# Best-32 attention with quads two to a turn behind the scores, and the state kernel in quarters

## The reference, cut to what matters

```python
s = q @ k.T / sqrt(32)              # per head, 128 queries x 4096 keys at a time
kth = top_k(s, 32)[..., -1:]
p = softmax(where(s >= kth, s, -inf))
c0 = mean_over_heads(p) @ context
K[d, l] = 2 * real(sum_n(dC[d, n] * exp(dtA[d, n] * l)))
```

## Time and profile before

| | us |
|---|---|
| median of 3 runs | 1250.7 (1249.63 to 1252.78) |
| profiled execution, time | 1249.94 |
| profiled execution, span | 1248.7 |
| PE busy | 1023.1 (82%) |
| DVE busy | 835.4 (67%) |
| ACT busy | 627.9 (50%) |
| POOL busy | 253.1 (20%) |

### The profile page before, as it was taken

The page is one execution under the profiler, slowest core; times in us unless marked ns, Lnnn a source line. Parts: engine busy times, 40 slices in busy tenths (PEclk is TensorE's granted clock), DMA queues, the critical chain, the costliest instruction groups (busy, mean ns, idle before and its releaser), DMA issues. The chain is left out here.

```text
span 1248.7 us, 20560 instructions
## 1 busy us (share of the span) xinstructions
PE 1023.1 (82%) x7560; PEld 624.6 (50%) x7560; DVE 835.4 (67%) x1812; ACT 627.9 (50%) x1014; POOL 253.1 (20%) x276
## 2 busy tenths in 40 slices
PE   6988589999999999868799782587787778973877
PEld 5877434444444444438455461335545456442564
DVE  5677689999999998036334559988485744533472
ACT  4434138787887888613311140799696882011100
POOL 1000488895000000000000010073434330000100
PEclk9999769999999999967799876667877789977855
DMA  6777522223222221010122270014521155003200
GB/s 207 273 260 270 185 66 77 78 77 84 76 76 80 76 76 39 10 53 1 52 89 76 80 187 5 1 56 115 139 78 51 39 156 186 0 1 84 68 1 17
DMA packets 97993, 110.63 MB, mean 89 GB/s; under 512 B 26475, under 2 KB 74404, under 8 KB 97892
## 3 DMA queue, kind: packets, MB, share of 16 engines
q1 hardware_dynamic: 95572, 108.52, 28.9%
q10 hardware_dynamic: 2320, 0.79, 0.3%
HBM read 79.77 MB, written 29.43 MB: 87 GB/s over the span
## 5 line engine op out<-in xcount | busy, mean ns | idle before, releaser
L806 ACT ACTIVATE pT<-bank 128x512 f32<-128x512 f32 x512 | 278.4, 597 | 94.6 <-PE bank L745 73.2
L827 DVE TENSOR_REDUCE rmax<-bank 128x2 f32<-128x1024 f32 x256 | 307.4, 1223 | 19.1 <-PE bank L713 18.1
L1547 PE MATMUL bank<-K1s,qs 97*128 97x512 f32 x256 | 137.2, 629 | 56.0 <-ACT below L1653 36.6
L757 PE MATMUL bank<-pT,V 128*17 128x256 f32 x2048 | 161.8, 388 | 4.7 <-ACT oT L812 4.6
L745 PEld LDWEIGHTS bank<-qs,ks 49*128 49x128 f32 x1024 | 78.1, 187 | 113.8 <-ACT pT L806 100.8
L1810 POOL TENSOR_TENSOR total<-total,work 128x1024 f32<-128x1024 f32 x40 | 94.7, 2375 | 194.9 <-ACT work L1662 194.5
L745 PE MATMUL bank<-qs,ks 49*128 49x256 f32 x1024 | 130.5, 333 | 2.5 <-ACT pT L806 0.5
L713 PE MATMUL bank<-ks,qs 49*128 49x512 f32 x512 | 111.2, 429 | 16.2 <-DMA ks<-k_parts_d 9.0
L1547 PEld LDWEIGHTS bank<-K1s,qs 97*128 97x128 f32 x256 | 61.1, 250 | 72.7 <-ACT below L1653 37.3
L1717 DVE MAX8 cand<-work 128x8 f32<-128x128 f32 x384 | 77.5, 279 | 0.0
L1662 ACT ACTIVATE work<-bank,ebias 128x1024 f32<-128x1024 f32 x48 | 53.6, 1120 | 31.7 <-PE bank L1550 31.7
(11 more groups left out here) (432 smaller groups left out, 1870.2 us busy)
## 6 DMA issues: line engine op xcount, KB each, us to landing
k_parts_d<-kparts SPq DMA_DIRECT2D x48, 512.0 KB, 3.6
ks<-k_parts_d SPq DMA_DIRECT2D x384, 64.0 KB, 2.2
K1s<-k_parts_d SPq DMA_DIRECT2D x96, 128.0 KB
cn<-in_ctx SPq DMA_DIRECT2D x32, 384.0 KB, 3.4
cx<-in_ctx SPq DMA_DIRECT2D x16, 384.0 KB
w<-in_L_ffn_w SPq DMA_DIRECT2D x32, 128.0 KB
w2e<-in_L_ffn_w SPq DMA_DIRECT2D x16, 128.0 KB
W<-in_L_xattn_W SPq DMA_DIRECT2D x2, 1024.0 KB, 7.4
```

Source lines behind the costliest of these rows:

```text
L757: t = pe.matmul(bank[32 * c:32 * c + VW, 7, a * S:(a + 1) * S], V[:, b * NCH + 4 * g + c, h, :], pT[:, (at + 2 * (c // 2) + a) % 8, c % 2 ...
L806: p_made.up(act.activation(pT[:, at % 8, :], bank[:, 4 + at % 3, :], ACT.Exp))
L827: max_read.up(dve.tensor_reduce(rmax[p % 2][:, :, qt, c], bank[:, b0:b0 + 2, :], AX.X, ALU.max))
L1547: m = pe.matmul(bank[:, b0 + c, :], qs1[0:NROW1, b * H1 + h, q], K1s[h][0:NROW1, keys], start=True, stop=(what == "new"))
```

## The change: what it does, and the diff

Seven edits, all in this stage. (1) `quads` becomes a table over quarters g = 4s + k: groups 0 and 1 get two quads per turn (quarters 0 and 2) in turns 6 to 9 and 10 to 13, group 2 gets two in turn 14, four in turn 15 and two in turn 16. (2) PE's loop puts the scores of a quarter first, then the weighing of the quad of the quarter before, then the turning of the next quarter's quad (where two quads follow on each other, of this quarter's). (3) The state kernel is made in four quarters, the first in bank 2 ahead of the turning in `prep_tensor`, the others one sixteenth per quarter turn in turns 0 to 2 in bank 7; its copies move accordingly. (4) `sum_over` moves from quarter 0 to quarter 1, with DVE's cast behind the candidates of quarter 1. (5) ACT runs `mark_below` before `sum_best`, and spreads `sum_best`, `log_sum` and `exp_bias` over quarters 1 to 3. (6) At the end DVE does one late add before `copy_c0` of group 2. (7) SP issues the context loads by the new table. The hunks that only move declarations (`kst`, the K flags) are left out below.

```diff
@@ -1316,6 +1316,26 @@
+    kst = [a.rearrange("p i d -> p (i d)").rearrange("p (a g) -> p a g", a=LA) for a in (xn[:, :, :], xT[:, :, :])]
+    K_made, K_copied, K_stored = flag("K_made"), flag("K_copied"), flag("K_stored")
+    def kernel_sixteenth(at, k_bank):
+        for i in range(4 * at, 4 * at + 4):
+            hs, g = slice(i // 32 * NSTATE, (i // 32 + 1) * NSTATE), i % 32
+            for c in range(2):
+                for q in range(4):
+                    m = pe.matmul(bank[32 * q:32 * q + LB, k_bank, i % 16 * LA:(i % 16 + 1) * LA],
+                                  Bp[c][hs, q, :, g], Ap[c][hs, q, :, g], start=(c == 0), stop=(c == 1))
+        if at % 4 == 3:
+            K_made.up(m)
+    def copy_kernel(n, k_bank):
+        act.wait_ge(*K_made.at(n + 1))
+        K_copied.up(act.copy(kst[n // 2][:, :, n % 2 * 16:n % 2 * 16 + 16].rearrange("p a g -> p g a"),
+                             bank[:, k_bank, :].rearrange("p (g a) -> p g a", a=LA)))
@@ -1343,6 +1363,9 @@
     def prep_tensor():
+        pe.wait_ge(*powers_made.at(1))
+        for at in range(4):
+            kernel_sixteenth(at, 2)
         pe.wait_ge(*ln_made.at(4 * 4))
@@ -1356,6 +1379,7 @@
         turn_scalar(4)
+        copy_kernel(0, 2)
         norm_scalar(4)
@@ -1443,13 +1465,19 @@
 
-    def quads(s):
-        grp, k = (s - 6) // H1, (s - 6) % H1
-        return [(grp, n) for n in ((0, 1), (2, 3, 4), (5, 6, 7), ())[k]] if s >= 6 and grp < NGRP - 1 else []
-    K_SHARE = (2, 1, 1)
+    quads = {}
+    for grp in range(NGRP - 1):
+        first = 4 * grp + 6
+        spots = [(first + j // 2, j % 2 * 2) for j in range(NQ)]
+        if grp == NGRP - 2:
+            spots = [(first, 0), (first, 2)] + [(first + 1, k) for k in range(4)] + [(first + 2, k) for k in range(2)]
+        for n, (s, k) in enumerate(spots):
+            quads[4 * s + k] = (grp, n)
+    K_FROM, K_BANK = 4, 7
 
@@ -1490,9 +1518,10 @@
                     vecs_in.up(sp.dma_start(vecs[:, k, :], row("L1_xattn_" + n).to_broadcast([P, D])), 16)
-            for _ in quads(s):
-                load_context(at)
-                at += 1
+            for k in range(4):
+                if 4 * s + k in quads:
+                    load_context(at)
+                    at += 1
         after_cut(LAST - 1)
@@ -1511,26 +1540,6 @@
     def best_tensor():
-        made = [0]
-        def kernel_share(n):
-            for at in range(4 * made[0], 4 * (made[0] + n)):
-                if at % 16 == 0:
-                    if at:
-                        pe.wait_ge(*K_copied.at(at // 16))
-                    else:
-                        pe.wait_ge(*powers_made.at(1))
-                        pe.wait_ge(*q1_low.at(H1))
-                hs, g = slice(at // 32 * NSTATE, (at // 32 + 1) * NSTATE), at % 32
-                for c in range(2):
-                    for q in range(4):
-                        m = pe.matmul(bank[32 * q:32 * q + LB, 7, at % 16 * LA:(at % 16 + 1) * LA],
-                                      Bp[c][hs, q, :, g], Ap[c][hs, q, :, g], start=(c == 0), stop=(c == 1))
-                if at % 16 == 15:
-                    K_made.up(m)
-            made[0] += n
@@ -1554,7 +1563,7 @@
                 pe.wait_ge(*over_in.at(t))
-            pe.wait_ge(*aT_made.at(sum(len(quads(s)) for s in range(t + 1))))
+            pe.wait_ge(*aT_made.at(total_turned.n))
             over_summed.up(pe.matmul(bank[0:1, 6, 0:1], over[:, :], ones[:, 0:1], start=True, stop=True))
@@ -1565,7 +1574,7 @@
                 pe.wait_ge(*aT_made.at(at))
-            pe.wait_ge(*over_in.at(min(NTL, 4 * grp + 6 + (n >= 2) + (n >= 5))))
+            pe.wait_ge(*over_in.at(over_summed.n))
             for c in range(4):
@@ -1585,24 +1594,28 @@
         for k in range(4):
+            if k == 1:
+                pe.wait_ge(*K_copied.at(1))
             if k == 2:
         pe.wait_ge(*minus_made.at(1))
-        for s in range(NTL + 1):
-            for k in range(4):
-                for what in pieces_of(s, k):
-                    piece(*what)
-                if k == 0 and 1 <= s <= NTL:
-                    sum_over(s - 1)
-                if s < len(K_SHARE):
-                    kernel_share(K_SHARE[s])
-                if 1 <= k <= len(quads(s)):
-                    turn_quad(*quads(s)[k - 1])
-                if 2 <= k <= len(quads(s)) + 1:
-                    weigh_quad(*quads(s)[k - 2])
-            if len(quads(s)) == 3:
-                weigh_quad(*quads(s)[2])
+        for g in range(4 * (NTL + 1)):
+            s, k = g // 4, g % 4
+            for what in pieces_of(s, k):
+                piece(*what)
+            if s and k == (s < NTL):
+                sum_over(s - 1)
+            if g < 12:
+                if g % 4 == 0:
+                    pe.wait_ge(*K_copied.at(g // 4 + 1))
+                kernel_sixteenth(K_FROM + g, K_BANK)
+            if g - 1 in quads:
+                weigh_quad(*quads[g - 1])
+            if g in quads and g - 1 in quads:
+                turn_quad(*quads[g])
+            if g + 1 in quads and g not in quads:
+                turn_quad(*quads[g + 1])
         piece("cut", LAST, 3)
@@ -1631,7 +1644,6 @@
             j = t % 2
-            act.wait_ge(*picked.at(t + 1))
             e_summed.up(act.activation(etop[:, :], top[j][:, :], ACT.Exp, bias=ntop[:, j:j + 1], accum_out=ssum[:, j:j + 1]))
@@ -1670,11 +1682,6 @@
-        def copy_kernel(n):
-            act.wait_ge(*K_made.at(n + 1))
-            K_copied.up(act.copy(kst[n // 2][:, :, n % 2 * 16:n % 2 * 16 + 16].rearrange("p a g -> p g a"),
-                                 bank[:, 7, :].rearrange("p (g a) -> p g a", a=LA)))
 
@@ -1686,23 +1693,25 @@
                         exps(t, piece)
-                if 1 <= s <= NTL:
+                if 1 <= s < NTL:
+                    if k % 2:
+                        mark_below(s - 1, k - 1, 2)
+                    if k == 1:
+                        sum_best(s - 1)
+                    if k == 2:
+                        log_sum(s - 1)
+                    if k == 3:
+                        exp_bias(s - 1)
+                if s == NTL:
+                    mark_below(s - 1, k, 1)
                     if k == 0:
                         sum_best(s - 1)
-                    if s == NTL:
-                        mark_below(s - 1, k, 1)
-                    elif k % 2:
-                        mark_below(s - 1, k - 1, 2)
-                    if k == 0:
                         log_sum(s - 1)
-                    if k == (s < NTL):
                         exp_bias(s - 1)
-                if s < len(K_SHARE):
-                    share = sum(4 * n for n in K_SHARE[:s]) + K_SHARE[s] * (k + 1)
-                    if share % 4 == 0:
-                        copy_kernel(share // 4 - 1)
-                if 1 <= k <= len(quads(s)):
-                    copy_quad(*quads(s)[k - 1])
+                if s < 3 and k == 3:
+                    copy_kernel(s + 1, K_BANK)
+                if 4 * s + k in quads:
+                    copy_quad(*quads[4 * s + k])
         exps(LAST, 3)
@@ -1781,9 +1790,8 @@
                     candidates(s, k)
-                if k == 0 and 1 <= s <= NTL:
+                if k == (s < NTL) and 1 <= s <= NTL:
                     over_to_sbuf(s - 1)
-                if k == (s < NTL) and 1 <= s <= NTL:
                     settle(s - 1)
@@ -1792,10 +1800,12 @@
                 copy_c0((s - 9) // H1)
-        for t, grp in ((LATE, NGRP - 2), (LAST, NGRP - 1)):
+        for t in (LATE, LAST):
             for k in range(4):
                 add_late(t, k)
-            copy_c0(grp)
+                if (t, k) == (LAST, 0):
+                    copy_c0(NGRP - 2)
+        copy_c0(NGRP - 1)
 
```

More of the change, by code:

```diff
@@ L1406, in build @@
     c0 = xn[:, :, 0:DC]
-    kst = [a.rearrange("p i d -> p (i d)").rearrange("p (a g) -> p a g", a=LA) for a in (xn[:, :, :], xT[:, :, :])]
     ctxn_d = ins["ctx_768"].rearrange("b (c p) d -> b p c d", p=P)
@@ L1419, in build @@
         "total_turned", "aT_made", "c0_made", "c0_copied", "tm_in", "tmask_made", "c0_turned", "c0T_made"))
-    K_made, K_copied, K_stored = flag("K_made"), flag("K_copied"), flag("K_stored")
     def home(t):
```

## The result

| us | before | after |
|---|---|---|
| median | 1251.74 (4 runs, 1249.63 to 1254.15) | 1218.18 (4 runs, 1213.21 to 1223.16) |
| profiled execution, time (span) | 1249.94 (1248.7) | 1213.21 (1211.7) |
| ratio | 1 | 0.9731, 95% interval 0.9684 to 0.9779 |

What follows compares the result with a forecast made beforehand. Neither engine was full: ACT and PE wait for each other in a chain of quad copy, turn, weigh, cut, exponentials. Savings 25.0 + 3.4 + 3.4 + 4.7 + 0.7 = 37.2 us gave 1213.5 us against the median; range 1202 to 1233.

Steps and rivals of the forecast that it cites:

- Part 1: Turns 6 to 14: two quads a turn behind the scores remove both holes; 14.1 us a turn, 25.0 us less.
- The bound of 13.1: Quad turns: ACT's work, turn 5's 12.1 us plus two quad copies of 0.46; reached if the clock is never low.
- the 0.9 for the clock: Quad turns: PE at 1.2 GHz a third of the time, 4.4 us in 13.1, costing ACT 0.9 us a turn.
- One sign named in advance: Turns 6 to 13: no idle time of ACT over 1.5 us before an L1662.
- rival (b): Quad turns: clock averages 0.64 as in turn 5, 15.5 us a turn; 1226, or 1231 us in all; chance 0.2.
- Rival (a): Quad turns: ACT bounds every turn at 13.1 us; nine turns save another 9.0, 1204.5 us in all; chance 0.2.
- Part 2: Overflow sum and its followers one quarter later in the turns: taken as 0, since ACT no longer asks at turn start.
- bounds of -1.9 and +5: Moving the overflow sum: gain at most ACT's 1.9 us wait for ntop, loss at most a 0.46 copy a turn.
- Part 3: Turns 15 and 16: 12.5 us against 15.9 and 13.5 against 16.9, each 3.4 us less.
- Part 4: State kernel: a quarter moves ahead of the prep's first turning, so tile 0's exact selection starts earlier; 4.7 us less.
- DVE alone: Start of tile 0's selection: limit if only DVE's flags and candidates set it, 6.2 us less.
- Part 5: The end: the last group's first quad no longer waits for DVE's add behind copy_c0(2); 0.7 us less.

## Why the prediction was right or wrong

**Part 1, turns 6 to 14: right, 26.5 us where 25.0 was forecast** (29 to 30 by the other two profiles of the changed kernel). The mechanism is shown from both sides: quads in neighbouring quarters bring the mutual waiting back, and a turn at a clock of 1.00 is at ACT's bound. A turn was put at 14.1; the profiles have two kinds from turn 7 on, 14.0 (clock 0.88) and 13.15 (clock 1.00), and turn 6 at up to 15.0 (0.77). The bound of 13.1 and the 0.9 for the clock were both on the mark, but the 0.9 was spread over all turns, where it is there or not. Its reason was wrong: the long pause was read as what costs the clock, yet with no pause of PE over 0.92 us turns 7 to 11 of the first profile all had a low stretch. So the size of the loss came out for a reason that the trace does not bear out, which is luck. One sign named in advance did not hold: ACT stood 1.79 us before an L1674 in turn 6, where nothing over 1.5 was expected. What the prediction did not part is what pays for what: the order, which it described first, is some 10 us, and the spreading, together with the sum out of its way, the larger part.

**The Trainium skill** speaks in "TensorE: Matmul & The Clock Gate", section "A second HAM failure mode: psum-queue depth-cycling", of short gaps between groups of matmuls that let the clock swing. The trace agrees that it does: 0.88 and 1.00 in turns with the same work. The price of rival (b), 15.5 us a turn, came only in turn 6 (15.0 at 0.77, in two of three profiles); in a turn at 0.88 ACT waits only 0.76 us, and turn 5's 0.64, from which (b) was worked out, did not carry over. Rival (a), every turn at 13.1, came true in one to five of turns 6 to 13, by run.

**Part 2, the sum a quarter later: the reading was wrong, and the 0 did no harm to the sum.** It was weighed as an edit by itself, with bounds of -1.9 and +5, and part 1 was costed as if the sum were in nobody's way. Without the move the sum meets the new quad of quarter 0 in bank 6, and 18.4 us are gone, far outside those bounds. For tile 0 the move costs 2 us.

**Part 3: turn 15 right (3.3 for 3.4), turn 16 wrong (0.4 for 3.4).** The failed step is "ACT was busy 13.92 of 16.9 in it, less one copy 13.5". It took the sum of ACT's busy time for the length of a turn whose last part is a chain: ACT marks the last quarter, PE cuts it, ACT takes its exponentials. There PE stands 2.24 us and then ACT 2.22 us for the cut, and a quad less does not shorten that. Of the two holes that the step took out, the one before the first exponentials (2.64 us) ends where turn 16 begins, so that it belongs to turn 15 and to its 3.3; the one before the last was 2.58 us and is still 2.22. ACT's busy time was forecast well (13.4 for 13.5), its 3.0 us of standing not. Some 0.9 of them are the clock: turn 16 took 15.5 us, at 1.00 instead of 0.91 to 0.93, with the idle work before the last cut and with eighteen idle matmuls in the turns.

**Part 4: right in kind, too small (6.2 for 4.7).** The delay of the turning was 2.05 us, as forecast (2.1). The mis-sized term is what stands between the turning and the first scores, which was left as it was: it is 3.7 us shorter (8.43 for 12.12), 2.9 of it in the projection and most of the rest in the turning, since both run at 2.4 GHz. Some 2.2 us of that were lost again behind it: turn 0 took 11.4 us instead of 10.6 at a clock of 0.50, where its steps had been priced from a row at 2.4 GHz, and DVE stood 1.14 us between the cast and the selection. That 6.2, the end of the range given for "DVE alone", was reached is chance: the flags came 1.5 us earlier after phase start, not 2.1 later, and DVE did wait for PE. Without the early quarter the selection starts 7.4 to 7.8 us later.

**Part 5: wrong (+2.6 for -0.7).** The wait for DVE's add is gone, but it was worth 0.4 us, not 0.7: the second turning needs bank 6 back, and ACT copies the first quad only behind its last exponentials (from these to the second turning 2.06 us before and 1.69 after). And the first quads of the last group run at 1.2 GHz: a weighing takes 2.56 us (998.10 to the next turning at 1000.66) where the earlier trace rows had 1.27 at 2.4. The step assumed the clock of before, 1.00 over this stretch. Filling the pause ahead of the last cut brings 2 us of that stretch, using it for quads 6.7.

**The sum** was 37.2, the touched stretches gave 32.8: +1.5 each from parts 1 and 4, -3.0 from turn 16, -3.3 from the end, -1.1 from turns 2 to 5, which were put at 0.

Open: why turns 3 to 5 are 0.9 us longer in this profile (0.2 in another of the same kernel); what decides whether a turn gets the clock of 0.88 or of 1.00; what the spreading would bring without the scores first, and what ACT's new order brings by itself (no run parts them); and how the gain of the spreading would divide if the sum stood in quarter 1 with the old spots, which was not tried.

## What to carry to other kernels

Where a single buffer is handed back and forth between two engines, leave a free step between two uses of it, and look at everything that passes through it, small sums too: with the quads moved to even quarters and the sum left in place, three quarters of the turns' gain were lost to one 1-column matmul in the same bank. Where the clock decides, put work that has to be done anyway into the pauses ahead of an expensive stretch: ahead of the projection and of the last cut it paid twice. And a last turn is costed along its chain, not by the busy time of its busiest engine.

## What was not expected of the hardware

After 6.2 us of small matmuls of the state kernel (64 rows, 32 columns), over which the granted clock averaged 0.73, it was at 1.00 all through the turning and the projection that followed, which took 7.08 us instead of 9.88 to 9.95; yet in turns 0 and 1, where PE is full with the same kind between pairs of scores, the clock was at 0.50 (724 to 745 us). The clock costs a turn less than its ratio: turns of the same work took 14.0 us at 0.88 and 13.15 at 1.00, since PE's slower work lies mostly beside ACT's. And the pause of 2.24 us before the last cut stood in every kernel that kept that end unfilled, but the cut behind it took 0.8 us for its first matmul in the changed kernel, 0.50 with eighteen idle matmuls in the turns long before, and 0.51 with the sum in quarter 0: a pause by itself does not say at which clock the next work runs.
